# Two cross-attention layers on one core: stores of the opening, the first norms, VectorE's order, and MLP sums in PSUM

## What is computed

```
# layer 0: 32 heads of 16, keys and values shared by groups of 4 heads
x = LN(softmax(q k^T / 4 + mask) v Wo + bo + x) * gamma + beta
# layer 1: two blocks of 16 heads of 128, each with one extra key and value
for i in (1, 2):
    h = LN(x); x = x + attention_i(h Wq_i, ctx Wk_i, ctx Wv_i) Wo_i + bo_i
h = LN(x); x = x + gelu(h W1 + b1) W2 + b2          # W1 is 512 x 2048
```

## Time and profile before

| | us |
|---|---|
| median of 3 runs (lowest, highest) | 2457.11 (2449.81, 2460.05) |
| the profiled execution | 2455.36 |
| its span, first to last instruction | 2453.3 |
| TensorE busy | 2311.3 (94%) |
| VectorE busy | 1401.8 (57%) |
| ScalarE busy | 998.9 (41%) |
| GpSimd busy | 766.4 (31%) |

### The profile page before, as it was taken

One profiled execution on the slowest core, in us unless ns is written; L12 is line 12 of the kernel. 1 busy time (PEld: TensorE's weight loads), 2 busy tenths in 40 slices (PEclk: granted clock), 3 DMA queues, 4 the chain that ended last, 5 costly groups with the idle time before them and its releaser, 6 DMA issues. The chain is left out here.

```text
span 2453.3 us, 36589 instructions
## 1 busy us (share of the span) xinstructions
PE 2311.3 (94%) x13464; PEld 2078.5 (85%) x13464; DVE 1401.8 (57%) x3146; ACT 998.9 (41%) x2195; POOL 766.4 (31%) x823
## 2 busy tenths in 40 slices
PE   6798899999999999998989979999999999999988
PEld 6576899998989999997877769899998999998976
DVE  4697645454565455456549955454546645455564
ACT  3695434243433333243239944343333424243420
POOL 3142332415141423313641341514142331405055
PEclk9899999999999999999999999999999999999999
DMA  8531323233323323234363213333232323233222
GB/s 275 166 98 33 96 86 104 87 94 114 99 86 96 96 82 110 81 99 142 129 202 98 73 49 92 116 95 97 85 96 90 106 81 100 91 101 103 83 72 80
DMA packets 134533, 250.46 MB, mean 102 GB/s; under 512 B 31151, under 2 KB 54831, under 8 KB 133335
## 3 DMA queue, kind: packets, MB, share of 16 engines
q10 hardware_dynamic: 44552, 126.75, 16.9%
q1 hardware_dynamic: 89807, 121.38, 16.3%
HBM read 223.19 MB, written 29.48 MB: 103 GB/s over the span
## 5 line engine op out<-in xcount | busy, mean ns | idle before, releaser
L671 POOL TENSOR_SCALAR wk_hi<-raw 128x512 fp32r<-128x512 f32 (+1 forms) x84 | 53.2, 634 | 902.5 <-DMA raw<-in_wk 745.3
L1412 ACT ACTIVATE probs<-scores,prm 112x376 f32<-112x376 f32 x256 | 147.0, 575 | 342.9 <-DVE prm L1805 342.9
L791 PE MATMUL pj_two<-ctx_hi,wk_hi 128*128 128x376 f32 x708 | 243.7, 344 | 6.3 <-DVE rr L1566 4.0
L1566 DVE TENSOR_TENSOR rr<-pj_two,rr 128x448 fp32r<-128x448 f32 (+2 forms) x223 | 146.9, 660 | 172.0 <-ACT rr L1174 171.8
L792 PE MATMUL pj_two<-ctx_lo,wk_hi 128*128 128x376 f32 x708 | 239.0, 338 | 0.0
L793 PE MATMUL pj_two<-ctx_hi,wk_lo 128*128 128x376 f32 x708 | 238.2, 337 | 0.0
L791 PE MATMUL pj_two<-pt_hi,nat 125*128 125x448 f32 x531 | 198.8, 374 | 9.3 <-issue 9.0
L673 POOL TENSOR_TENSOR wb_lo<-raw,wb_hi 128x512 fp32r<-128x512 f32 x152 | 199.9, 1315 | 12.7
L1568 DVE SCALAR_TENSOR_TENSOR k_lo<-pj_two,cur,k_hi 128x375 fp32r<-128x375 f32 x167 | 101.3, 607 | 173.0 <-ACT k_hi L1176 172.4
L793 PE MATMUL pj_two<-pt_hi,nat 125*128 125x448 f32 x531 | 195.4, 368 | 0.0
L792 PE MATMUL pj_two<-pt_lo,nat 125*128 125x448 f32 x531 | 195.3, 368 | 0.0
(11 more groups left out here) (278 smaller groups left out, 6581.9 us busy)
## 6 DMA issues: line engine op xcount, KB each, us to landing
nat<-nat_scratch ACTq DMA_DIRECT2D x256, 384.0 KB, 3.7
raw<-in_wq SPq DMA_DIRECT2D x72, 256.0 KB, 3.2
raw<-in_wo SPq DMA_DIRECT2D x72, 256.0 KB, 2.6
raw<-in_wk SPq DMA_DIRECT2D x64, 256.0 KB, 3.8
raw<-in_wv SPq DMA_DIRECT2D x64, 256.0 KB, 4.2
raw<-in_w SPq DMA_DIRECT2D x64, 256.0 KB, 2.9
nat_scratch<-rr ACTq DMA_DIRECT2D x7, 1536.0 KB, 6.3
k_hi<-keys_scratch SPq DMA_DIRECT2D x32, 188.0 KB, 2.6
```

Source lines behind the costliest of these rows:

```text
L671: nc.gpsimd.tensor_scalar(hi, src, 1.0, 0.0, ALU.mult, ALU.add).then_inc(split_hi, 1)
L791: nc.tensor.matmul(dst, l_hi, r_hi, start=first, stop=False)
L1412: nc.scalar.activation(probs[0:L, h, 0:SK], scores[n % SCR][0:L, 0:SK], ACT.Exp, bias=neg_max[0:L, h:h + 1], accum_out=row_sum[0:L, h:h + ...
L1566: i = nc.vector.tensor_tensor(dst, src, hi.bitcast(F32), ALU.subtract)
```

## The change

- **Opening's order and stores.** Half 0: q0 before k2, k3 behind q3, n2 before c2. Half 1: q3 and k3 later. SyncE: the two small bias stores first, the queries' load ahead of the mask, stores of q1, q2 and q3 ahead of k3; in half 1 k2's stores ahead of q3's. ScalarE: the natural contexts' stores of batches 1, 3 and 2 come after k2, q1 and q3. `pt0` begins with the buffer in `rr` in both halves, and ScalarE waits for place 1 at n = 1, the queries at n = 4, place 0 at n = 16, place 2 and the bias rows at n = 24.
- **Norms' boundary.** The keys of head 0 go before the first normalised batch. GpSimd takes the low parts of h; for batches 2 and 3 VectorE scales (`scaled`, four pieces) and ScalarE only copies the high parts (`h_parts`, two pieces).
- **Order in the groups.** As in the diff: low parts before normalisations on VectorE, high parts before the exponential of head 3 on ScalarE.
- **MLP.** The second product of all four blocks adds up in the four `q_banks`; VectorE adds each bank to `xa` once a half. Half 1's output leaves in four DMAs. Half 1's first scores wait for the four additions of half 0, and the first transposes that use `pj_two` wait for the opening's last unit.

```diff
     if half == 0:
-        order = "c0 n0 c1 k0 n1 k1 c2 n2 vt0 x0 k2 q0 vt1 v0 c3 n3 q1 vt2 v1 k3 q2 vt3 v2 q3 v3"
+        order = "c0 n0 c1 k0 n1 k1 n2 c2 vt0 x0 q0 k2 vt1 v0 c3 n3 q1 vt2 v1 q2 vt3 v2 q3 k3 v3"
     else:
-        order = "k0 q0 k1 q1 vt0 q2 vt1 v0 k2 q3 vt2 v1 k3 vt3 v2 v3"
+        order = "k0 q0 k1 q1 vt0 q2 vt1 v0 k2 vt2 v1 q3 vt3 v2 k3 v3"
...
-        return x[0:1] + keys[0:2] + x[1:2] + keys[2:4] + qa[0:1] + x[2:3] + qa[1:3] + x[3:4] + qa[3:]
+        return keys[0:1] + x[0:1] + keys[1:3] + x[1:2] + keys[3:] + x[2:3] + qa[0:2] + x[3:4] + qa[2:]
...
                     store_keys0(2, *pre_split("k", 2))
-                    store_queries0(0, *pre_split("q", 0))
+                    load_queries0(0, 0)
 
                     sp.wait_ge(pj_free, pre_freed("n", 2, SC - 1) + PJ)
+                    sp.wait_ge(ctx_ready, HB - 1)
                     load_mask()
-                    load_queries0(0, 0)
+                    store_queries0(1, *pre_split("q", 1))
                     load_keys0(0, 2)
...
+                def first_rest(b):
+                    for k in range(2):
+                        c = slice(2 * k, 2 * k + 2)
+                        pool.wait_ge(ln_hi, (nl * HB + b) * 2 + k + 1)
+                        nc.gpsimd.tensor_tensor(h_lo[:, c, b * L:(b + 1) * L],
+                                                tmp[1][:, 2 * k * L:(2 * k + 2) * L].rearrange("p (c l) -> p c l", c=2),
+                                                h_hi[:, c, b * L:(b + 1) * L].bitcast(F32), ALU.subtract).then_inc(ln_lo, 1)
+                first_normed(0)
+                first_normed(1)
+                first_rest(0)
+                first_normed(2)
+                first_rest(1)
+                first_normed(3)
+                first_rest(2)
+                first_rest(3)
...
                     for b in range(HB):
-                        out_part(mpj, hf * WO_H + 1 + NG + m, mu["o", b], b, (qo_hi, qo_lo), ready2)
+                            last = three(q_banks[b][0:L, :], [q[:, h, b * L:(b + 1) * L] for q in (qo_hi, qo_lo)],
+                                         (w_hi["o"][:, h, :], w_lo["o"][:, h, :]), m == 0 and h == 0,
+                                         m == MLPG - 1 and h == HPG - 1)
...
-                    if n == (1, 4)[hf]:
+                    if n == 1:
+                        stored(1)
+                    if n == 4:
                         for t in q0_out:
                             act.wait_ge(t, (hf + 1) * 32)
...
                         keys1(b, 1)
+                        split_p(b - 1, 0)
+                        split_p(b - 1, 1)
                         if b == 1:
                             exps1(0, 3)
-                        split_p(b - 1, 0)
-                        split_p(b - 1, 1)
...
                             max1(0, 3)
-                            norm1(0, 2)
                         split_p(b - 1, 0)
                         split_p(b - 1, 1)
                         if b == 1:
+                            norm1(0, 2)
                             norm1(0, 3)
...
-                        norm1(b, 0)
                         split_p(b - 1, 2)
                         split_p(b - 1, 3)
+                        norm1(b, 0)
...
-                    rest(0)
                     post_normed(2)
-                    keys1(0)
                     moments_of(2, 1)
                     moments_of(3, 0)
+                    x_read(0)
...
-                    rest(2)
-                    rest(3)
+                    scaled(nl, 2, gpj + gu["x", 2])
+                    scaled(nl, 3, gpj + gu["x", 3])
...
+                for b in range(HB):
+                    dve.wait_ge(mlp_summed, hf * HB + b + 1)
+                    nc.vector.tensor_tensor(xa[0:L, b, :], q_banks[b][0:L, :], xa[0:L, b, :], ALU.add).then_inc(sums_added, 1)
```

More of the change, by code:

```diff
@@ L142 @@
 MLP_MID = [len(names) for names in MLP_HEADS]
-MU = [places(names + [("o", b) for b in range(HB)]) for names in MLP_HEADS]
+MU = [places(names) for names in MLP_HEADS]
 MLP_U = [len(u) for u in MU]
@@ L734, in _ @@
                 if hf == 1:
-                    pool.wait_ge(pj_ready, PJ_AT[0]["end"])
+                    pool.wait_ge(mlp_summed, HB)
                     empty_rows()
@@ L763, in _, with first_normed @@
                 nl = hf * NL
-                for b in range(HB):
+                def first_normed(b):
                     pool.wait_ge(ln_inv, nl * HB + b + 1)
@@ L1341, in _, with stored @@
                 for n in range(NT):
-                    if n == (1, 4)[hf]:
+                    def stored(place):
+                        batches = [NAT_N[hf][b] + 1 for b in range(HB) if NAT_AT[hf][b] == place]
+                        act.wait_ge(nat_out[place], 16 * batches[-1])
+                    if n == 1:
+                        stored(1)
+                    if n == 4:
                         for t in q0_out:
                             act.wait_ge(t, (hf + 1) * 32)
-                    if n == (4, 1)[hf]:
-                        for i in range(2 if hf else 3):
-                            stored = [NAT_N[hf][b] + 1 for b in range(HB) if NAT_AT[hf][b] == i]
-                            act.wait_ge(nat_out[i], 16 * stored[-1])
                         if hf == 0:
-                            act.wait_ge(bx_out, 48)
-                            act.sem_inc(w_free["o"], 1)
+                            act.wait_ge(setup_bv, 3 * HPG)
+                    if n == 16:
+                        stored(0)
+                    if n == 24 and hf == 0:
+                        stored(2)
+                        act.wait_ge(bx_out, 48)
+                        act.sem_inc(w_free["o"], 1)
                     if n >= 8 and n % 4 == 0:
@@ L1357, in _ @@
                         two = n // 2
-                        move(pt0[(n // 4 + hf) % 2][0][0:KC, n % 4 - 1:n % 4 + 1, :], twos[two % 2][0:KC, :, 0:SC * L],
+                        move(pt0[(n // 4 + 1) % 2][0][0:KC, n % 4 - 1:n % 4 + 1, :], twos[two % 2][0:KC, :, 0:SC * L],
                              two_ready, two0 + two + 1, mid=two_mid)
@@ L1954, in inverse, with x_read @@
                         nc.vector.reciprocal(rstd[0:L, b:b + 1], std[0:L, b:b + 1]).then_inc(ln_inv, 1)
-                    def rest(b):
+                    def x_read(b):
                         dve.wait_ge(ln_hi, (nl * HB + b) * 2 + 2)
@@ L1978, in l0_norms @@
                     added(3)
+                    keys1(0)
                     moments_of(1, 1)
@@ L2025, in _ @@
                             mlp_operands(m + 1)
-                    if hf == 0 and m == MLPG - 1:
-                        split_x(1)
-                        wk0_rest(1)
-                    for b in range(HB):
-                        out_part(mpj, mu["o", b], b, stat=False)
-                        if b == 0 and hf == 0:
-                            split_ctx(1, m, mpj + mu["n", SC - 1] + 1)
+                    if hf == 0:
+                        split_ctx(1, m, mpj + mu["n", SC - 1] + 1)
+                        if m == MLPG - 1:
+                            split_x(1)
+                            wk0_rest(1)
+                for b in range(HB):
+                    dve.wait_ge(mlp_summed, hf * HB + b + 1)
+                    if b == HB - 1:
+                        dve.sem_inc(w_free["o"], 1)
+                    nc.vector.tensor_tensor(xa[0:L, b, :], q_banks[b][0:L, :], xa[0:L, b, :], ALU.add).then_inc(sums_added, 1)
 def kernel(**inputs):
```

64 lines of the change are left out of this document (39 added, 25 removed).

## The result

The changed kernel takes 2413.64 us (2412.11 to 2424.32, 4 runs) beside 2456.31 for the kernel before on the same chip: a ratio of 0.9837, 95% interval 0.9821 to 0.9852. That is 1.6% less, and 11.6 us more than the 2402 predicted, inside the range of 2388 to 2424. The profiled execution took 2412.11 us with a span of 2410.1.

What follows compares the result with a forecast made beforehand. It took TensorE to be the bound, with matmuls for 2311.3 of 2453.3 us, and counted only its idle time and clock. Savings 18 + 12 + 21.5 + 1 + 2 = 54.5 us from 2457.1 gave 2402, range 2388 to 2424.

Steps and rivals of the forecast that it cites:

- forecast case: Whole kernel: all five parts bring their predicted savings, 54.5 us together, giving 2402 us; chance 0.62.
- the first rival: Opening of half 0 stays bound by its transfers: only 6 of its 18 us come, 2414 us; chance 0.15.
- Groups, -21.5: The 16 groups: VectorE's new order saves 21.5 us, 0.8 of TensorE's 26.9 us of waits there; ends 5 and 27.
- The rival in which the gain only moves there: Groups: the wait moves to the normalisations, so only 5 of 21.5 us come, 2419 us; chance 0.14.
- Norms, -12: Norms after the first attention: 6 us saved in each half, 12 in all, 1 us a half from clock; ends 7 and 15.
- the last queries of the norms' boundary starting 6 us sooner after the w0 products: Norms' boundary: a sign, 6 us in size, that would show the forecast right.
- Opening of half 0, -18: Half 0's opening: 10 us from earlier first scores, 7 from the second wait, 1 from clock; ends 6 and 22.
- the second wait falls from 7.8 to about 1: Half 0's opening: TensorE's wait on ScalarE, held by the queries' stores, shrinks, saving 7 us.
- MLP and half 1's opening, -1: MLP sums in PSUM save 4 us in half 0, but half 1's opening leaves only 1; ends -4 and 5.
- The loss at the queries' stores: Half 1: rival in which MLP sums save nothing and 4 us are lost there, 2407 us; no chance of its own given.
- End, -2: Kernel's end: the last output in four stores of 224 KB, three under matmuls, saves 2 us; ends 0.5 and 3.
- The slower rival: Groups: GpSimd stretches two adjacent normalisations and the clock drops, 3.3 us a group more, 2477 us; chance 0.02.

Runs made afterwards that it cites:

- setup_wait_later: Changed kernel with, in half 0, ScalarE's wait for the twelve small bias-row operations before unit 8 instead of unit 4; 2412.2 us, ratio .9826.
- half0_tuned: Changed kernel with setup_wait_later's edit, half 0's bias rows and mask issued earlier, q3's store before the zeroing store, last two natural stores later; 2411.5 us, ratio .9825.
- changed_again: The changed kernel run once more, unchanged, in five rounds; 2413.9 us, ratio .9848 to the kernel before.
- half1_order_of_before: Changed kernel with half 1's order of units and stores put back as before (q3's store ahead of k2's, k3 made earlier); 2412.9 us, ratio .9833.
- groups_alone: Kernel before with only the order of VectorE's and ScalarE's work in the groups changed; 2438.8 us, ratio .9927.

## Why the prediction was right, and where it was not

The forecast case came in its larger part, short of its sum: 43.2 us in the profiled execution instead of 54.5. The measured 2413.6 is also the number of the first rival, 2414, but not its make-up: there the opening was to bring 6 us and everything else its full share, while it brought 11.4 and the rest of the loss is in half 1. By its steps, in the profiled execution and over all kernels of the table:

- **Groups, -21.5: -21.0.** The sum was right, its make-up not, so that the two agree within 0.5 us is partly luck. I took 0.8 of all three kinds of wait. What went is all of pt_lo and issue (8.1 + 12.9 = 21.0) and nothing of the normalisations (5.9, now 6.2). In all TensorE's idle time fell by 19.4 us, since short gaps came in, and its busy time by 1.6. That the normalisations end sooner and TensorE arrives sooner by as much fits their unchanged row. The rival in which the gain only moves there is refuted; its row was to pass 12 us.
- **Norms, -12: -11.4** (-10.3 over all kernels). From w0 to the first group's scores it is 5.3 and 6.2 us less, where 6 and 6 were put down. But the sign "the last queries of the norms' boundary starting 6 us sooner after the w0 products" did not come: they start 3.7 and 4.5 us sooner after w0 (243.47 - 207.22 = 36.3 us against 258.51 - 218.60 = 39.9 in half 0), and the stretch from them to the first group's scores gave 1.6 us in either half, where 1 was put down for the clock.
- **Opening of half 0, -18: -11.4** (-11.6 over eight kernels). First scores at 59.1, "near 58 to 60" was right. The step that failed is "the second wait falls from 7.8 to about 1": it is 4.33, and the mask adds 2.55 at the second score. It counted ScalarE's full wait as 6 us of work later and the queries' stores as sooner by what no longer stands before them. But q3's store went out at 62.07, behind a store that held SyncE 5.83 us, and with `setup_bv` the change puts at unit 4 a wait for the bias rows that I had not costed at all. setup_wait_later shows that the queries' stores alone cost these 4 us (4.32), with the store ahead of theirs down to 1.04 us. The bias rows alone were not run; at 71.67 against 70.98 they would cost as much there. half0_tuned, which moves both, has 1.96 us left. The mask took 13.6 us to land, not 11.2, as its own part of the same stretch.
- **MLP and half 1's opening, -1: +3.2** in the changed kernel (-4.1 + 1.7 + 4.7 + 0.9), -1.1 in changed_again. The MLP of half 0 brought its 4 us (3.6 over all kernels), that of half 1 nothing, as said. The loss at the queries' stores is the rival's: I took 1 us of 4 as kept, with "2 to 3 us later than needed"; ScalarE stood 4.10 us, over the 3 that I had put down as a sign of being wrong, and the attention is 4.7 us longer, 4.0 of them by half1_order_of_before for that store. The second query weights cost 3.35 us, where I saw 1 to 2. The MLP in half 1 differed by 4.1 us between two executions of the same kernel, with a granted clock of 0.83 in one stretch of the first (1.00 there in changed_again):

```profile
2319.00:2339.00 20.00, 15.58 (x70) 11.31 (x69) 9.43 (x10) 3.04 (x5) 8.19 (x8) 0.83 0.20 66
```

- **End, -2: -2.5.**
- **The slower rival** needed the two adjacent normalisations stretched. Of 256 normalisations 27 took over 1 us before and 12 do now; the mean fell from 518 to 476 ns, and the granted clock in the groups is 1.00 in both. They are stretched less often in the new order, not more. The Trainium skill (SBUF — State Buffer, section "Who interferes with whom") has VectorE in a two-port mode and GpSimd block each other for a whole instruction; the stretched ones fit that, and no run here isolates it.

The forecast was right for its reason in two of five parts, the norms and the end; in the groups the number came with another make-up. -18 and -1 were the two that rest on when a transfer lands, and both were too kind. Two numbers of the forecast do not follow from its own working: the squares give a lower end of 2402 - 8.5, near 2394, and not 2388, and the first four cases add up to 0.96 for faster and not 0.94. Neither changes the outcome.

## What to carry to other kernels

Where two waits stand one behind the other on the same engine, cost them together: the first one's gain is stood again at the second until that goes too (1.7 us alone, 7.0 together). When a wait is moved, list every condition that is moved with it, and for each the queue that serves it; at unit 4 two arrived 0.7 us apart, so taking one away helped little. And read a change of several parts by stretches, beside its median: here the attention of half 1, where it was left as it was, repeated within 0.2 us, while the medians had intervals of 3 to 6 us.

## What the runs showed of the hardware

- Half 0's opening ran differently with the same order of transfers. Over eight kernels (in setup_wait_later one wait of ScalarE is moved) the mask was issued at 46.22, 46.33, 48.02, 48.34, 48.52, 48.60, 48.63 and 52.26 us, and held VectorE 0, 0, 3.98, 4.33, 0, 5.67, 6.73 and 8.84 us. The issue time alone does not decide it (48.52 held nothing), and the changed kernel and changed_again, 3.98 and 6.73, are the same program.
- A load of 128 KB issued 0.39 us later took 5.7 and not 2.2 us to land, beside the first keys' stores.
- The time in which a single issue holds SyncE differs likewise: in the same eight kernels the same zeroing store (240 KB) took 0.94 to 5.83 us, and where it was short a queries' store beside it was longer (1.04 and 3.89 us in setup_wait_later, 0.94 and 4.83 in half1_order_of_before). The issue of the last queries' store ended at 61.8 to 66.6 us all the same.
- How much the clock takes differs between executions. The span times one less its mean granted clock is 36 us before, 24 in the changed kernel and 48 in groups_alone, whose 22 us less of idle time gave only 13.5 us of span: its busy time is 2319.4 us and not 2311.3.
